# Three-layer CIN on one core: the first three passes take their layers in another order, and the initial loads follow it

## The reference

```python
def cin(x0, params, split_flags):            # (W1,b1),(W2,b2),(W3,b3); True, True, False
    x, results = x0, []
    for (W, b), split in zip(params, split_flags):
        z = einsum('bhd,bmd->bhmd', x, x0).reshape(B, h * 32, D)
        xk = relu(einsum('oc,bcd->bod', W, z) + b[None, :, None])
        if split:
            x, xk = xk[:, :64], xk[:, 64:]
        else:
            x = xk
        results.append(xk)
    return sum(concatenate(results, axis=1), axis=2) @ Wo.T + bo
```

## Time and profile before

| | |
|---|---|
| median of three runs | 482.07 us |
| profiled execution, its own time | 480.3 us |
| its span, first to last instruction | 478.5 us |
| TensorE busy | 443.9 us, 93% |
| VectorE / ScalarE / GpSimd busy | 424.8 / 310.7 / 408.4 us |
| HBM read / moved by DMA | 61.48 / 78.42 MB |

### The profile page before, as it was taken

The page is one execution under the profiler, slowest core; times in us unless marked ns, Lnnn a source line. Parts: engine busy times, 40 slices in busy tenths (PEclk is TensorE's granted clock), DMA queues, the critical chain, the costliest instruction groups (busy, mean ns, idle before and its releaser), DMA issues.

```text
span 478.5 us, 5975 instructions
## 1 busy us (share of the span) xinstructions
PE 443.9 (93%) x1601; PEld 302.7 (63%) x1601; DVE 424.8 (89%) x489; ACT 310.7 (65%) x383; POOL 408.4 (85%) x147
## 2 busy tenths in 40 slices
PE   0758599999999999999999999999999999999994
PEld 0325276766667676666767676666767676677672
DVE  1556599999999999999999999999999999999994
ACT  1224667686858677676858677676857677686650
POOL 0107499998999999999999999999999999999991
PEclk9998599999999999999999999999999999999999
DMA  8999999989695959689695959689594954630100
GB/s 210 244 232 223 256 226 209 210 191 205 137 227 120 219 126 221 136 186 209 136 231 112 223 124 222 136 191 204 136 232 112 222 122 98 133 79 10 44 0 1
DMA packets 23232, 78.42 MB, mean 164 GB/s; under 512 B 5939, under 2 KB 5939, under 8 KB 18996
## 3 DMA queue, kind: packets, MB, share of 16 engines
q1 hardware_dynamic: 23220, 78.28, 74.5%
HBM read 61.48 MB, written 0.00 MB: 128 GB/s over the span
## 4 chain that ended last, share of the span: by engine, by line
PE 81%; DMA 6%; DVE 5%; issue 2%; ACT 2%; SPq 2%; POOL 1%; DVEq 0%
PE y_ps L706 25%; PE y_ps L694 14%; PE y_ps L712 14%; PE y_ps L696 14%; PE y_ps L702 7%; DVE z L534 4%; PE y_ps L718 3%; DMA a_rep<-x_sb 3%; DMA w_raw<-w_dram 2%; DMA shifted<-xt_dram 1%; ACT zh L423 1%; PE y_ps L672 1%; POOL zl L481 1%; SPq L329 1%; PE y_ps L698 1%
## 5 line engine op out<-in xcount | busy, mean ns | idle before, releaser
L481 POOL TENSOR_TENSOR zl<-z,zh 128x1024 fp32r<-128x1024 f32 (+1 forms) x141 | 406.6, 2919 | 48.6 <-ACT zh L423 48.2
L534 DVE TENSOR_TENSOR z<-a_ps,b_fac 128x1536 f32<-128x1536 f32 x254 | 269.6, 1083 | 25.7 <-PE y_ps L718 13.2
L423 ACT ACTIVATE zh<-z 128x1024 fp32r<-128x1024 f32 (+1 forms) x141 | 176.8, 1254 | 113.2 <-DVE z L534 112.9
L712 PE MATMUL y_ps<-zl,w_high 128*128 128x512 f32 x332 | 154.6, 559 | 1.9 <-POOL zl L481 1.9
L694 PE MATMUL y_ps<-zh,w_high 128*128 128x512 f32 x332 | 131.9, 397 | 10.1 <-ACT zh L423 10.1
L696 PE MATMUL y_ps<-zh,w_low 128*128 128x512 f32 x332 | 130.8, 394 | 0.0
L706 PE MATMUL y_ps<-z,w_raw 128*128 128x512 f32 x254 | 129.5, 591 | 0.0
L712 PEld LDWEIGHTS y_ps<-zl,w_high 128*128 128x128 f32 x332 | 62.4, 189 | 70.1 <-issue 61.8
L694 PEld LDWEIGHTS y_ps<-zh,w_high 128*128 128x128 f32 x332 | 62.8, 189 | 25.4 <-issue 6.4
L696 PEld LDWEIGHTS y_ps<-zh,w_low 128*128 128x128 f32 x332 | 63.0, 190 | 13.8
L706 PEld LDWEIGHTS y_ps<-z,w_raw 128*128 128x128 f32 x254 | 47.9, 189 | 10.6
(11 more groups left out here) (45 smaller groups left out, 164.8 us busy)
## 6 DMA issues: line engine op xcount, KB each, us to landing
b_fac<-xt_dram SPq DMA_DIRECT2D x60, 512.0 KB, 9.0
shifted<-xt_dram SPq DMA_DIRECT2D x64, 256.0 KB, 4.9
a_rep<-x_sb SPq DMA_DIRECT2D x96, 128.0 KB, 3.0
shifted<-xt_dram SPq DMA_DIRECT2D x64, 128.0 KB, 5.2
a_rep<-x_sb SPq DMA_DIRECT2D x64, 64.0 KB, 2.7
b_fac<-xt_dram SPq DMA_DIRECT2D x8, 256.0 KB, 10.7
w_raw<-w_dram SPq DMA_DIRECT2D x2, 640.0 KB, 13.1
w_raw<-w_dram SPq DMA_DIRECT2D x2, 384.0 KB, 12.5
```

The lines of the kernel that those rows point to most:

```text
L423: nc.scalar.activation(zh[:, slot, 0:end - native, :], z[:, slot, native:end, :], ACT.Copy).then_inc(zh_ready, 1)
L481: nc.gpsimd.tensor_tensor(zl[:, slot, 0:end - native, :], z[:, slot, native:end, :], zh[:, slot, 0:end - native, :].bitcast(F32), ALU.subtract
L534: return nc.vector.tensor_tensor(dst, factor.unsqueeze(1).to_broadcast(list(dst.shape)), others, ALU.mult)
L712: mm = nc.tensor.matmul(y, wh[layer][:, w, :], zl[:, slot, t, :], start=False, stop=end_here)
```

## The change

Pass 1 takes layer 2 (chunk 0), then layer 1 (chunk 1); pass 2 takes layer 3 (chunk 0), layer 1 (chunk 2), layer 2 (chunk 1). From pass 3 on the order is 1, 2, 3 as before. In the new numbers G1 to G4 are layer 2 of chunk 0, G5 is layer 1 of chunk 1, G6 to G9 layer 3 of chunk 0, G10 layer 1 of chunk 2, G11 to G14 layer 2 of chunk 1, and G15 (layer 1) and G16 to G19 (layer 2 of chunk 2) begin pass 3. The loads are queued in another order, and ScalarE's and VectorE's steps between groups are placed anew for passes 1 and 2.

```diff
+LAYERS = {1: (2, 1, 3), 2: (3, 1, 2)}
+W_PARTS = {1: (0,), 2: (1, 0), 3: (0, 1)}
 def layers_of(i):
-    return [layer for layer in (1, 2, 3) if 0 <= i - layer + 1 < NCHUNK]
+    return [layer for layer in in_order(i) if exists(i - layer + 1)]
+def in_order(i):
+    return LAYERS.get(i, (1, 2, 3)) if isinstance(i, int) else (1, 2, 3)
+def positions(i):
+    return [FIRST[layer] + g for layer in in_order(i) for g in range(GROUPS[layer])]
...
-        z_fifth = (results3, x_out[2])
+        z_fifth = results3
...
             sp.dma_start(cols_sb[:], cols).then_inc(cols_loaded, 16)
-            load_x(1)
             load_w(2, w2, 0)
             load_b(0, ((0, 4, b0_loaded[0]),))
             def body(i):
+                if i_is(i, 0):
+                    spread(1, 0)
+                    load_b(0, ((4, 8, b0_loaded[1]),))
+                    load_w(2, w2, 1)
+                    load_x(1)
+                    load_w(3, w3, 0)
+                    return
+                if i_is(i, 1):
+                    spread(2, 0)
+                    load_w(3, w3, 1)
+                    load_x(2)
+                    spread(1, 1)
+                    load_b(1)
+                    sp.dma_start(bo_sb[:], bo).then_inc(bo_loaded, 16)
+                    load_x(3)
+                    return
                 if exists(i):
                     spread(1, i)
-                if i_is(i, 0):
-                    load_b(0, ((4, 8, b0_loaded[1]),))
-                    load_w(2, w2, 1)
-                if i_is(i, 1):
-                    load_w(3, w3, 0)
-                    load_w(3, w3, 1)
+                if i_is(i, 2):
+                    load_b(2)
                 if exists(i + 2):
                     load_x(i + 2)
                 if exists(i - 1):
                     spread(2, i - 1)
                 if exists(i + 1):
                     load_b(i + 1)
-                if i_is(i, 0):
-                    sp.dma_start(bo_sb[:], bo).then_inc(bo_loaded, 16)
...
 ScalarE, body(i), for pos in positions(i), after the group's own steps
+                    if i_is(i, 1):
+                        if pos == 2:
+                            a_to_psum(2, 1, 0)
+                            round_w(2, 1)
+                        if pos == 4:
+                            round_w(2, 0)
+                            x_to_psum(1)
+                            y_to_sbuf(2, 0)
+                        if pos == 0:
+                            y_to_sbuf(1, 1)
+                            round_w(3, 0)
+                            a_to_psum(3, 0, 0)
+                            a_to_psum(3, 1, 0)
+                        continue
+                    if i_is(i, 2):
+                        if pos == 5:
+                            round_w(3, 1)
+                        if pos == 7:
+                            a_to_psum(2, 0, 1)
+                            x_to_psum(2)
+                        if pos == 0:
+                            a_to_psum(2, 1, 1)
+                        if pos == 2:
+                            y_to_sbuf(1, 2)
+                        if pos == 4:
+                            a_to_psum(2, 0, 2)
+                            x_to_psum(3)
+                        continue
...
+                    if pos == 1 and i_is(i, 3):
+                        y_to_sbuf(2, 1)
...
 VectorE, body(i)
+                    if i_is(i, 1):
+                        if pos == 2:
+                            pool12(0)
+                            split_w(2, 1)
+                        if pos == 0:
+                            subtract(i, *here[0])
+                            split_w(2, 0)
+                            split_w(3, 0)
+                            break
+                        continue
+                    if i_is(i, 2):
+                        if pos == 5:
+                            split_w(3, 1)
+                        if pos == 8:
+                            pool12(1)
+                        continue
```

More of the change, by code:

```diff
@@ L120, in dve_tiles @@
 def dve_tiles(i):
-    order = [(layer, g) for layer in (1, 2, 3) if exists(i - (layer - 1)) for g in range(GROUPS[layer])]
+    order = [(layer, g) for layer in layers_of(i) for g in range(GROUPS[layer])]
     return [(layer, g, 0 if is_native(groups_before(i) + k) else BY_DVE[layer][g])
@@ L130, in groups_through @@
     if isinstance(i, int):
-        return groups_before(i) + sum(GROUPS[k] for k in layers_of(i) if k <= layer)
+        here = layers_of(i)
+        return groups_before(i) + sum(GROUPS[k] for k in here[:here.index(layer) + 1])
     return groups_before(i) + FIRST[layer] + GROUPS[layer]
@@ L415, in body @@
                 here = {step[0]: (step, k) for k, step in enumerate(steps(i))}
-                for pos in range(PER_ITER):
+                for pos in positions(i):
                     if pos in here and not is_native(here[pos][0][3]):
@@ L444, in body @@
-                    if pos in (2, 4) and i_is(i, 2):
-                        round_w(3, pos // 2 - 1)
+                    if i_is(i, 0):
+                        if pos == 0:
+                            y_to_sbuf(1, 0)
+                        continue
[13 more added lines that the diff above has]
+                        continue
@@ L446, in body @@
                     if pos == 0 and i_is(i, NCHUNK):
                         act.wait_ge(z_native_ready, groups_before(i))
[L448 removed]
+                    if pos == 0 and exists(i - 1):
                         a_to_psum(2, 1, i - 1)
+                    if pos == 1 and i_is(i, 3):
+                        y_to_sbuf(2, 1)
                     if pos == 3 and exists(i - 2):
@@ L489, in split_w @@
             def split_w(layer, part):
-                dve.wait_ge(w_rounded[layer], part + 1)
+                dve.wait_ge(w_rounded[layer], W_PARTS[layer].index(part) + 1)
                 tiles = split_part(layer, part)
@@ L563, in product @@
                         factor = a_ps[:, half, :]
-                        dve.wait_ge(a_in_psum[layer][half], c + 1)
+                        dve.wait_ge(a_in_psum[layer][half], c if layer == 2 and half == 0 else c + 1)
                 if not isinstance(q, int) or q >= RING:
@@ L603, in body @@
                 here = {s[0]: (s, k) for k, s in enumerate(steps(i))}
-                for pos in range(PER_ITER):
+                before = None
+                for pos in positions(i):
                     if pos in here:
                         product(i, *here[pos])
[L608 to L620, removed]
+                    if before in here and before in ZX_BANK and not is_native(here[before][0][3]):
+                        subtract(i, *here[before])
+                    before = pos
+                    if i_is(i, 0):
+                        if pos == 0:
+                            dve.wait_ge(wq_rounded, 1)
+                            nc.vector.tensor_tensor(wq[Q:2 * Q, 0, :], wq_raw[Q:2 * Q, 0, :],
+                                                    wq[Q:2 * Q, 0, :].bitcast(F32), ALU.subtract).then_inc(wq_made, 1)
+                            split_w(1, 0)
+                        continue
[3 more added lines that the diff above has]
+                            split_w(2, 1)
+                        if pos == 0:
+                            subtract(i, *here[0])
+                            split_w(2, 0)
+                            split_w(3, 0)
+                            break
+                        continue
+                    if i_is(i, 2):
[3 more added lines that the diff above has]
+                            pool12(1)
+                        continue
+                    if pos == (4 if i_is(i, 3) else 1) and exists(i - 2):
@@ L674, in body @@
                             pe.wait_ge(z_fifth_ready, c + 1)
-                            mm = nc.tensor.matmul(y, wq_raw[:, 1, :], z_fifth[c][:], start=False, stop=True)
+                            mm = nc.tensor.matmul(y, wq_raw[:, 1, :], z_fifth[:], start=False, stop=True)
                         mm.then_inc(group_used, 1)
                         continue
-                    if i_is(i, 2) and layer == 1:
+                    if i_is(i, 1) and layer == 1:
                         pe.wait_ge(w_split[1], 1)
                         pe.wait_ge(wq_made, 1)
-                    for part, first in enumerate((1 if layer == 2 else 0, 2)):
-                        if layer > 1 and i_is(i, layer - 1) and g == first:
-                            pe.wait_ge(w_split[layer], part + 1)
+                    if layer == 2 and (i_is(i, 1) and g == 2 or i_is(i, 2) and g == 0):
+                        pe.wait_ge(w_split[2], i)
+                    if layer == 3 and i_is(i, 2) and g in (0, 2):
+                        pe.wait_ge(w_split[3], g // 2 + 1)
                     by_pool = end - native - QUARTER[layer]
```

25 lines of the change are left out of this document (7 added, 18 removed).

## The result

The changed kernel takes 493.28 us (median of four runs, 491.94 to 494.79) against 482.26 of before: ratio 1.0217, interval 1.0179 to 1.0255. That is 11.0 us slower; I had forecast 7.1 slower and a time of 489.2, and the measured one lies 0.7 us above my range. The side, the places and the order of the waits were those forecast; the largest term was about half of what it is.

A forecast was written before the change was run, and what follows sets the result against it. The prediction took the start, the first 80 us, to be bound by the DMA backlog. Its terms, +2.45 for the start and +4.65 for the late `b_fac`, gave 482.07 + 7.1 = 489.2 us, range 483.5 to 492.6.

The forecast's parts named there:

- Part 5: Third chunk's `b_fac`, issued behind G10's spread, lands at 91.3; G16 idles 3.0 us, GpSimd's lead is lost: +4.65 us.
- two other restarts: G1 and G5, each given 1.9 us extra for the lower clock after a gap.
- Parts 1 to 4: Start through G14: engine chains and gaps replace transfer waits; G6 at 56.2, G15 at 87.15 against 84.70: +2.45 us.
- part 4: G6 to G14: moved steps lie beside TensorE's work, G10 ends at 75.45, G15 starts at 87.15, still +2.5 us.
- (A): Rival: chunk 2's `b_fac` is in time, only the start's +2.45 stays: 484.5 us, chance 0.15.
- (B): Rival: both `b_fac` loads run at about twice 216 GB/s on a short queue: -1.15, 480.9 us, chance 0.09.
- (C): Rival: queue not empty by 18.7 us, first spread lands at about 27, all 1.6 later: 490.8 us, chance 0.08.

The follow-up runs named there:

- Run 3: Changed kernel with loads of the first three passes, including the third chunk's `b_fac`, issued into the times when the queue was empty: 485.78 us.
- run 6: Changed kernel with the late `b_fac` load put behind one more x load: 499.6 us.
- run 2: Changed kernel with ScalarE taking layer 2's sum of chunk 1 out of PSUM before G16's zh instead of behind it: 491.89 us.
- run 4: Changed kernel with VectorE making G15's last low part before it waits for G16's `b_fac`: 492.95 us.
- run 10: Changed kernel with idle matmuls in TensorE's gaps before G1, G5 and G6: 494.21 us.
- run 12: run 9 with idle matmuls added in the gaps before G1 and G6 and at the end: 480.69 us.
- run 11: Kernel before the change with three idle matmuls in its last gap: 481.04 us, ratio 0.998.
- run 9: run 8 with half of chunk 1's x queued already in the initial batch: 480.54 us, ratio 0.9967.
- Runs 7: Changed kernel with ScalarE's order in pass 1 changed: G5 rounded before layer 2's sum is taken out, third layer's first weight part rounded earlier: 493.85 us.
- run 8: Changed kernel with the edits of Run 3 and Runs 7 together, and `a_to_psum(2, 0, 2)` moved to position 0 of pass 3: 481.85 us.

## Why the prediction was wrong where it was wrong

**The mechanism held.** The gaps of G1, G3, G5 and G6 and the chain ScalarE-VectorE-ScalarE that takes the place of the transfer wait before G6 are in the trace, each group up to G6 starting within 1 us of the forecast, and the third chunk's `b_fac` is the largest loss, as forecast. Run 3 removes the loss by the transfers alone and run 6 scales it.

**Part 5, +4.65, was mis-sized: it measured 8.9** (7.5 in the second profile). This is the step that failed: the term for the third chunk's `b_fac` had the late landing and left out most of what stands behind it. Three things were missing. (a) I let G16 restart at full speed after a 3 us gap, though I had priced two other restarts; it took 2.8 us (1.6 in the second profile). My sum let GpSimd's low part of G17 set the end, but in the trace that was done by 103.9 and TensorE, still working off the slow group, took it at 106.06. (b) G16 started at 98.4 and not at 96.6, when its zh was made, for two reasons that cover each other (runs 2 and 4): `y_to_sbuf(2, 1)` at position 1 of pass 3 stands behind that zh on ScalarE, and G15's last low part stands behind G16's product on VectorE. I followed the first to the spread that it starts and not to the bank that it releases, and took G15 for finished. (c) From G10's end (77.15) to the landing (94.1) it is 17.0 us where I had 15.85: ScalarE was in a zh when G10 ended (0.5 us), and the load took 12.7 instead of 12.0. The forecast's 3.0 us until G16 became 3.0 + 1.1 + 1.8, and instead of 1.65 behind it there were 2.9.

**Parts 1 to 4, +2.45, measured +4.1** (5.9 in the second profile). Up to G6 0.8 us were added. They are not G1's: nearly all of it ran at the lower clock (6.6 us, I had 5.35), but G2 still waited 0.69 us behind it, for `b_fac`. They are made up of small terms: G0 took 5.64 us instead of 5.27, so the spread began 0.24 later, `b_fac`'s second part was there at 29.24 and not at 28.85, and from VectorE's product to G2 I had counted 1.2 us where the 1.38 that I used for G1 was right. The rest is in G6: I gave it 5.2 us and a wait of 0.4, but it lasts 6.4 (57.01 to 63.39), since its last matmul waits for VectorE's `subtract`, behind `split_w(3, 1)` and G7's product. In every run with the new order it lasts 6.37 to 6.43 us, also where its first matmuls ran at the full clock (runs 10 and 12). That the moved `split_w(3, 1)` lies beside TensorE's work was the sentence of part 4 that failed. My terms from G6 to G10 also add up to 75.26 and not to 75.45.

**The clock at the very end** adds 1.4 us between the two profiled executions; on average it should add less, since run 11 won 1.0 us there in before. I had compared with the profile of before as if its 480.3 against the median of 482.07 were a plain offset.

**Rivals.** (A), `b_fac` in time, and (B), quick loads on a short queue, fell: the load on an empty queue ran as slowly as in rows 8. (C), the queue not empty by 18.7, fell: it was empty from 17 on, which turned out to be a cost as well as a gain (run 9).

**The rate of the late load.** It moved 204 GB/s at a share of 0.96 from 81.4 to 94.1 us. The Trainium skill's ceiling of 435 GB/s for the fabric (page "DMA: Bandwidth & Descriptors", section Specifications) isn't approached by this load. Other transfers come nearer: in the kernel before, 52 to 54 us moved 368 GB/s at a share of 1.00. So the busy share alone doesn't give the rate; which transfer it is has to be looked up too.

## What to carry to other kernels

Where the transfers bound the start, count the queue's idle time before you reorder it: here each load that came sooner was paid for with empty queue in front of a wait, and the bill came at the last load of the backlog. When a step is moved, follow each thing that it releases (the data, the bank, the next load in the queue), not only the one it was moved for. And price a gap with the restart behind it, unless another engine's chain is as long as the slow group.

## What was not expected of the hardware

VectorE's `split_w` (both operands in SBUF) takes 0.96 us alone and up to 2.15 beside GpSimd in this kernel. The changed kernel's timelines of VectorE and GpSimd:

```profile
46.89 2.15 DVE L535 TENSOR_TENSOR w_low<-w_raw,w_high 128x768 fp32r<-128x768 f32 x1
53.69 0.96 DVE L535 TENSOR_TENSOR w_low<-w_raw,w_high 128x768 fp32r<-128x768 f32 x1 [4.65 <-ACT w_high L428]
58.26 1.88 DVE L535 TENSOR_TENSOR w_low<-w_raw,w_high 128x768 fp32r<-128x768 f32 x1 [1.28 <-ACT w_high L428]
...
45.84 2.38 POOL L524 TENSOR_TENSOR zl<-z,zh 128x1024 fp32r<-128x1024 f32 x1 [3.47 <-ACT zh L445]
56.95 2.38 POOL L524 TENSOR_TENSOR zl<-z,zh 128x1024 fp32r<-128x1024 f32 x1 [8.73 <-ACT zh L445]
```

GpSimd's two subtractions end at 48.22 and 59.33, the two long splits at 49.04 and 60.14, each 0.8 us later; the one at 53.69 had no GpSimd beside it and took its 0.96. The long ones waited for the end of GpSimd's instruction. Runs 7 and 8 bear this out: there the same split began later beside GpSimd's subtraction, took 1.24 and 1.37 us, and again ended 0.8 us behind it (53.50 against 52.68, 55.77 against 54.96). The Trainium skill says the same, on the page "SBUF — State Buffer", section "SBUF: two separate sides": a VectorE instruction with two SBUF inputs and a GpSimd one that reads SBUF exclude each other for the whole of an instruction. VectorE's products with one operand in PSUM are not slowed: one of two tiles took 1.21 us at 68.70, beside GpSimd, and 1.22 at 54.56, with GpSimd idle. That the late `split_w(3, 1)` delays G6 by about 0.9 us of its 6.4 follows from these rows; no run moved it out of GpSimd's way.

The length of the slow phase after a gap varies from execution to execution: G1, after the same gap of 5.12 us, took 6.63 in one profile and 5.37 in the other. Single runs of one kernel scatter by 1 to 3 us, and this is one part of it.
